# A Mamba mixer on one core: decays from two float32r parts, a shorter step-size chain, the skip moved three steps, one buffer for tokens and second norm

## The reference

```
mod = (silu(c) @ wmod) -> sa, ca, ga, sb, cb, gb      # per sequence, 256 each
h   = layernorm(x) * (1 + ca) + sa
x   = x + ga * attn(h);   h = layernorm(x) * (1 + cb) + sb
x   = x + gb * ffn(h)

attn(h):  xn = layernorm(h) * ln_w + ln_b              # the second norm
          z, xBC, dt = split(xn @ in_proj_w)           # 512, 768, 32 columns
          dt  = softplus(dt + dt_bias)                 # the step size, 32 heads
          xBC = silu(causal_conv(xBC, 4 taps));  x_ssm, B, C = split(xBC)
          # per head h, over time t:
          state = state * exp(dt*A) + dt * outer(x_ssm, B);   y = state @ C
          y = (y + D_skip * x_ssm) * silu(z)           # the skip
          y = y * rsqrt(mean(y^2)) * rms_w;  out = y @ out_proj_w + h
          out = out + relu(layernorm(out) @ m1 + b1) @ m2 + b2
```

## Time and profile before

| | |
|---|---|
| median of 3 runs | 3185.61 us |
| the profiled execution, its own time | 3180.88 us |
| its span | 3179.2 us |
| mean granted TensorE clock | 0.943 of full |
| TensorE busy over the span | 2799.2 us (88%) |
| VectorE busy | 1839.9 us (58%) |
| ScalarE busy | 1384.6 us (44%) |
| GpSimd busy | 678.1 us (21%) |

### The profile page before, as it was taken

The page is one execution under the profiler, slowest core; times in us unless marked ns, Lnnn a source line. Parts: engine busy times, 40 slices in busy tenths (PEclk is TensorE's granted clock), DMA queues, the critical chain, the costliest instruction groups (busy, mean ns, idle before and its releaser), DMA issues. The chain is left out here.

```text
span 3179.2 us, 46142 instructions
## 1 busy us (share of the span) xinstructions
PE 2799.2 (88%) x16998; PEld 2086.3 (66%) x16998; DVE 1839.9 (58%) x3504; ACT 1384.6 (44%) x2394; POOL 678.1 (21%) x716
## 2 busy tenths in 40 slices
PE   0488888888888888869999799999999999999999
PEld 0354555455555555458888687887878787878787
DVE  4688888888888888746767433333333333333332
ACT  0566666666666666536555322222222222222221
POOL 5022222222222222210000122222222222222221
PEclk6799989998999899879999899999999999999999
DMA  3010101010101010035211100000000000000000
GB/s 125 29 35 20 35 20 35 20 35 20 35 21 35 21 35 11 28 104 208 70 62 64 48 13 7 11 14 16 14 16 14 16 14 16 14 16 14 16 14 8
DMA packets 104858, 107.06 MB, mean 34 GB/s; under 512 B 35897, under 2 KB 98617, under 8 KB 102977
## 3 DMA queue, kind: packets, MB, share of 16 engines
q1 hardware_dynamic: 99520, 103.81, 10.1%
q10 hardware_dynamic: 5120, 0.19, 0.1%
HBM read 71.41 MB, written 40.94 MB: 35 GB/s over the span
## 5 line engine op out<-in xcount | busy, mean ns | idle before, releaser
L1597 PE MATMUL fbank<-hid,fw 128*128 128x512 f32 x4096 | 962.3, 395 | 0.0
L1597 PEld LDWEIGHTS fbank<-hid,fw 128*128 128x128 f32 x4096 | 766.1, 187 | 187.0
L1747 DVE TENSOR_TENSOR hid<-fhf,hid 128x512 fp32r<-128x512 f32 x384 | 264.9, 690 | 704.3 <-POOL hid L1704 704.3
L1704 POOL TENSOR_SCALAR hid<-fhf 128x512 fp32r<-128x512 f32 x384 | 271.1, 706 | 1040.2 <-ACT fhf L1676 760.8
L808 ACT ACTIVATE mh<-ebank 128x512 f32<-128x512 f32 x512 | 302.0, 598 | 415.0 <-PE ebank L663 413.8
L1121 DVE SCALAR_TENSOR_TENSOR mh<-mh,gm 128x512 f32<-128x512 f32 x512 | 403.2, 794 | 1.8 <-ACT mh L808 1.8
L663 PE MATMUL ebank<-cright,cleft 102*128 102x512 bf16 x512 | 211.1, 413 | 64.1 <-ACT cin L847 28.9
L1676 ACT ACTIVATE fhf<-fbank,sh2c 128x512 f32<-128x512 f32 x128 | 88.0, 688 | 382.4 <-PE fbank L1597 382.4
L676 PE MATMUL yin<-mh,xpad 128*32 128x128 f32 x4096 | 230.5, 300 | 27.1 <-DVE mh L1121 26.6
L650 PE MATMUL ebank<-ah,win 128*128 128x512 f32 x640 | 246.7, 425 | 7.1 <-ACT cin L847 6.6
L1676 ACT ACTIVATE fhf<-fbank,sh1c 128x512 f32<-128x512 f32 x128 | 88.1, 688 | 320.8 <-PE fbank L1597 320.6
(11 more groups left out here) (180 smaller groups left out, 4380.1 us busy)
## 6 DMA issues: line engine op xcount, KB each, us to landing
fx<-x_d SPq DMA_DIRECT2D x17, 512.0 KB, 3.9
xs<-in_x SPq DMA_DIRECT2D x16, 512.0 KB, 4.3
h_d<-in_h SPq DMA_DIRECT2D x16, 512.0 KB, 5.4
o_d<-o SPq DMA_DIRECT2D x16, 512.0 KB, 2.9
mo<-o_d SPq DMA_DIRECT2D x16, 512.0 KB, 3.8
mx<-in_x SPq DMA_DIRECT2D x16, 512.0 KB, 4.8
x_d<-mx SPq DMA_DIRECT2D x16, 512.0 KB, 2.8
fw<-h_d SPq DMA_DIRECT2D x2, 4096.0 KB, 15.2
```

The lines of the kernel that those rows point to most:

```text
L1597: mm = pe.matmul(bank[banks.slot(key)][:], w[:, k, m * P:(m + 1) * P].bitcast(dt), h[:, k, :].bitcast(dt), start=(k + n == 0), stop=(k == ...
L1704: pool.tensor_scalar(hid[i % 2][0][:, m, :], hf[j % 3][:], 1.0, 0.0, ALU.mult, ALU.add)\
L1747: dve.tensor_tensor(hid[i % 2][1][:, m, :], hf[j % 3][:], hid[i % 2][0][:, m, :].bitcast(F32), ALU.subtract).then_inc(c_lo.sem, 1)
```

## The change

The decay data have two float32r parts in place of three bf16: `cum` rounded to float32r, and the rest (one copy and one subtraction, where there were five instructions). `pick`, `cleft` and `cright` become float32r with 64, 69 and 69 rows in place of 96, 102 and 102, and the constant for masked exponents is -32768. The DMAs into them are 8 per block and 2 per chunk in place of 12 and 3, of 512 bytes a row in place of 256. GpSimd writes the constants once in float32, and ScalarE copies them into the float32r tiles. `chain` has 17 steps in place of 20. `skip` runs at i = 6 of its own chunk, not at i = 3 of the next. The second norm is written over the tokens (`nrm = xs`), so a load waits until TensorE's transposes of the norm before have been read out.

```diff
-LEFT = 99 + P // STRIP - 1
-NEVER = -30000.0
+LEFT = 2 * NH + 2 + P // STRIP - 1
+NEVER = -32768.0
-CHAIN = SERIES + 13
+CHAIN = SERIES + 10
-    pick = sb("pick", [96, QI, P], BF16)
-    cleft = [sb(f"cleft{j}", [LEFT, NC, P], BF16) for j in range(2)]
-    cright = [sb(f"cright{j}", [LEFT, NH, P], BF16) for j in range(2)]
+    pick = sb("pick", [2 * NH, QI, P], F32R)
+    cleft = [sb(f"cleft{j}", [LEFT, NC, P], F32R) for j in range(2)]
+    cright = [sb(f"cright{j}", [LEFT, NH, P], F32R) for j in range(2)]
@@ prologue, scalar
+            act.wait_ge(s_fill, FILLED)
+            nc.scalar.activation(pick[:], pick_f[:], ACT.Copy)
+            for j in range(2):
+                nc.scalar.activation(cleft[j][:], left_f[:].unsqueeze(1).to_broadcast([LEFT, NC, P]), ACT.Copy)
+                nc.scalar.activation(cright[j][:], right_f[:], ACT.Copy)
@@ prologue, gpsimd
-            for j in range(3):
-                v = pick[:].rearrange("k q (h d) -> k (q h) d", d=HD)
+            v = left_f[2 * NH:LEFT, :]
+            pool.affine_select(out=v, in_=v, compare_op=ALU.is_ge, fill=0.0, base=STRIP,
+                               pattern=[[1, P]], channel_multiplier=-STRIP)
+            v = right_f[2 * NH:LEFT, :, :]
+            pool.affine_select(out=v, in_=v, compare_op=ALU.is_ge, fill=NEVER, base=STRIP,
+                               pattern=[[0, NH], [1, P]], channel_multiplier=-STRIP).then_inc(s_fill, 1)
+            for j in range(2):
+                pool.wait_ge(s_fill, 3 + j)
+                v = pick_f[:].rearrange("k q (h d) -> k (q h) d", d=HD)
                 pool.affine_select(out=v, in_=v, compare_op=ALU.not_equal, fill=1.0, base=-NH * j,
                                    pattern=[[-1, NH], [0, HD]], channel_multiplier=1)
-                for r in range(2):
-                    v = cright[r][0:96, :, :]
-                    last = pool.affine_select(out=v, in_=v, compare_op=ALU.not_equal, fill=-1.0,
-                                              base=-NH * j, pattern=[[-1, NH], [0, P]], channel_multiplier=1)
...
+                v = right_f[0:2 * NH, :, :]
+                pool.affine_select(out=v, in_=v, compare_op=ALU.not_equal, fill=-1.0, base=-NH * j,
+                                   pattern=[[-1, NH], [0, P]], channel_multiplier=1).then_inc(s_fill, 1)
-    nrm = sb("nrm", [P, NC, D])
+    nrm = xs
-    parts = [sb(f"parts{r}", [P, 3, P], BF16) for r in range(2)]
+    parts = [sb(f"parts{r}", [P, 2, P], F32R) for r in range(2)]
@@ mixer, sync
+                if i + 2 < BLOCKS:
+                    released(sp, ("nT", i + 1, KD - 1))
+                    load(i + 2)
                 decay_right(NC * i + 2)
...
-                if i + 3 < BLOCKS:
-                    sp.wait_ge(c_norm.sem, c_norm.at(0, i + 3))
-                    load(i + 3)
@@ mixer, scalar
-                if i == 3 and has_chunk(q - 1):
-                    skip(q - 1)
+                if i == 6 and has_chunk(q):
+                    skip(q)
@@ mixer, vector, chain
                 elif step == SERIES + 8:
                     mark(dve.tensor_copy(p_[:, 0, :], cum[:]))
-                elif step == SERIES + 9:
-                    mark(dve.tensor_tensor(crest[:, 0, :], cum[:], p_[:, 0, :], ALU.subtract))
-                elif step == SERIES + 10:
-                    mark(dve.tensor_copy(p_[:, 1, :], crest[:, 0, :]))
-                elif step == SERIES + 11:
-                    mark(dve.tensor_tensor(crest[:, 1, :], crest[:, 0, :], p_[:, 1, :], ALU.subtract))
                 else:
-                    dve.tensor_copy(p_[:, 2, :], crest[:, 1, :]).then_inc(c_cum.sem, 1)
+                    dve.tensor_tensor(p_[:, 1, :], cum[:], p_[:, 0, :].bitcast(F32), ALU.subtract)\
+                        .then_inc(c_cum.sem, 1)
```

More of the change, by code:

```diff
@@ L314, in mixer @@
     h_mh = Handover(sem, "mh", groups, MH)
-    h_left = Handover(sem, "cleft", list(blocks), 2, fills=16 * 3 * NC, both=False)
-    h_right = Handover(sem, "cright", list(chunks), 2, fills=48, both=False)
+    h_left = Handover(sem, "cleft", list(blocks), 2, fills=16 * 2 * NC, both=False)
+    h_right = Handover(sem, "cright", list(chunks), 2, fills=32, both=False)
     c_yread = Count(sem, "yin_read", 0)
@@ L467, in _ @@
             pool.memset(tri[:], 1.0)
[L468 to L472, removed]
+            pool.memset(pick_f[:], 0.0)
+            pool.memset(left_f[:], 1.0)
+            pool.memset(right_f[:], 0.0).then_inc(s_fill, 1)
             pool.wait_ge(s_fill, 1)
@@ L478, in _ @@
             pool.wait_ge(s_fill, 2)
-            for j in range(3):
-                v = pick[:].rearrange("k q (h d) -> k (q h) d", d=HD)
+            v = left_f[2 * NH:LEFT, :]
[7 more added lines that the diff above has]
+                v = pick_f[:].rearrange("k q (h d) -> k (q h) d", d=HD)
                 pool.affine_select(out=v, in_=v, compare_op=ALU.not_equal, fill=1.0, base=-NH * j,
                                    pattern=[[-1, NH], [0, HD]], channel_multiplier=1)
-                for r in range(2):
-                    v = cright[r][0:96, :, :]
-                    last = pool.affine_select(out=v, in_=v, compare_op=ALU.not_equal, fill=-1.0,
-                                              base=-NH * j, pattern=[[-1, NH], [0, P]], channel_multiplier=1)
[L487 to L498, removed]
+                v = right_f[0:2 * NH, :, :]
+                pool.affine_select(out=v, in_=v, compare_op=ALU.not_equal, fill=-1.0, base=-NH * j,
+                                   pattern=[[-1, NH], [0, P]], channel_multiplier=1).then_inc(s_fill, 1)
+            pool.wait_ge(s_fill, FILLED)
     xs = sb("xs", [P, NC, D])
@@ L595, in decay_right @@
                     made(sp, ("eb", q - 2, NG - 1))
-                for j in range(3):
-                    sp.dma_start(cright[q % 2][96 + j:97 + j, :, :],
-                                 parts[q // NC % 2][NH * (q % NC):NH * (q % NC) + NH, j, :])\
+                for j in range(2):
+                    sp.dma_start(cright[q % 2][2 * NH + j:2 * NH + j + 1, :, :].bitcast(F32),
+                                 parts[q // NC % 2][NH * (q % NC):NH * (q % NC) + NH, j, :].bitcast(F32))\
                         .then_inc(h_right.full(q), 16)
@@ L605, in decay_left @@
                 for c in range(NC):
-                    for r in range(3):
-                        sp.dma_start(cleft[j % 2][NH * r:NH * (r + 1), c, :],
-                                     parts[j % 2][NH * c:NH * (c + 1), r, :]).then_inc(h_left.full(j), 16)
+                    for r in range(2):
+                        sp.dma_start(cleft[j % 2][NH * r:NH * (r + 1), c, :].bitcast(F32),
+                                     parts[j % 2][NH * c:NH * (c + 1), r, :].bitcast(F32)).then_inc(h_left.full(j), 16)
             load(0)
[L611 to L616, removed]
+            released(sp, ("nT", 0, KD - 1))
+            load(1)
+            decay_left(0)
+            decay_right(0)
             for i in blocks:
                 decay_right(NC * i + 1)
+                if i + 2 < BLOCKS:
+                    released(sp, ("nT", i + 1, KD - 1))
+                    load(i + 2)
                 decay_right(NC * i + 2)
@@ L685, in state_decay @@
                 for f in range(QI):
[L686 removed]
+                    mm = pe.matmul(o[:, f * P:(f + 1) * P], pick[:, f, :], cleft[q // NC % 2][0:2 * NH, q % NC, :],
                                    start=True, stop=True)
@@ L1190, in _ @@
                         low(j, AL_AT.index(n))
-                    if 0 <= n - CHAIN_FROM < CHAIN // CHAIN_PER:
-                        for step in range(CHAIN_PER):
-                            chain(j, CHAIN_PER * (n - CHAIN_FROM) + step)
+                    for step in range(CHAIN_PER * (n - CHAIN_FROM), CHAIN_PER * (n - CHAIN_FROM + 1)):
+                        if 0 <= step < CHAIN:
+                            chain(j, step)
                     if n == WV_AT:
```

5 lines of the change are left out of this document (4 added, 1 removed).

## The result

The changed kernel takes 3280.57 us, median of 4 runs (3278.43 to 3283.45), against 3186.28 us in the same session: 1.0289 times as long, 95% interval 1.0267 to 1.0312. It is slower by 94 us; 14.7 were forecast.

The account below looks back on a forecast made before the run. TensorE, with ScalarE's readings in its loop, was taken to pace the blocks. Terms -15 - 1 - 24.8 - 4.2 + 38.7 + 3 + 5 + 11 + 2 = +14.7 on 3185.6 gave 3200 us, range 3160 to 3232.

Parts of the forecast that it names:

- Prologue, -15: Before the blocks: fewer GpSimd selects let VectorE's small instructions and the split of `w_in` run faster, saving 15 us.
- Skip, its price: Steps 6, 14 and 22: the skip delays ScalarE's readings, 1.29 us each; +38.7 for 6 and 14, +3 for 22.
- The wait for `cin`: Sign at the exponent products: TensorE waits near 2.25 us, 30 times, some 65 us in all where it was 28.9.
- Skip, its gain: Block ends and starts: waits tied to the skip go, 1.65 us per end (-24.8) and 0.28 per start (-4.2).
- Float32r decays, +16: TensorE in the blocks: longer weight loads, +5 at steps 0, 4 and 5, +11 for `state_decay` at 9, 17 and 25.
- Rival C: Blocks: products of 128 columns at float32's price, +22, 3222 us, or more low-clock stretches; chance 0.18.
- B: Rival, TensorE's weight loads: they hide behind other products, so no change, 3184 us; chance 0.12.
- The clock, no price: Mixer: longer waits at steps 6 and 14 could bring more stretches at 1.2 GHz; nothing for it in the sum.
- Blocks with the waits filled: Sign in the mixer: blocks take 1.9 us longer than before.
- A: Rival, blocks: VectorE sets the pace, TensorE's slack swallows the skip's 38.7 us, 3162 us; chance 0.20.
- D: Rival, block ends: the wait for TensorE's `intra` replaces the skip's, the 24.8 us go, 3225 us; part of Rival C's chance.

Follow-up runs that it names:

- E2: Kernel before the change with only the skip moved to i = 6 of its own chunk; 3207.1 us.
- E5: Changed kernel, with TensorE repeating the transpose of B eight times more at steps 6, 14 and 22, results unused; 3221.2 us.
- E4: Kernel before the change, bf16 parts kept, with constants written once in float32 and copied by ScalarE, and the skip at i = 5 of its own chunk; 3119.9 us.
- E10: Kernel before the change with only the constants written once in float32 and copied by ScalarE; 3177.2 us.
- E11: E3 with ten float32r products of unused result at step 29, where TensorE waits for the Silu; 3211.3 us.
- E7: E4 with ten float32r products of unused result at step 29, where TensorE waits for the Silu; 3143.3 us.
- E1: Changed kernel with the skip put back at i = 3 of the next chunk; 3220.1 us.
- E3: Changed kernel with the skip at i = 5 of its own chunk, one step earlier; 3197.9 us.
- E8: E4 with the second norm written over the tokens and the changed kernel's order of loads of x; 3121.9 us.

## Why the prediction was wrong

TensorE's steps, from one exponent product to the next, in us, even block 6 and odd block 7 of each profile; some steps are left out, `all` is the whole block:

```
step    before      E2          after       E5          E4
  0   5.74  6.56  5.49  5.39  6.39  6.41  5.89  5.38  4.60  5.14
  5   3.11  3.11  2.89  2.89  4.64  2.89  2.89  2.89  2.89  2.88
  6   2.24  2.24  3.39  3.39  3.40  3.40  3.40  3.40  2.24  2.24
  7   2.18  2.18  2.18  2.55  4.04  2.29  2.29  2.29  2.18  2.18
  8   3.32  3.32  3.32  4.49  4.49  3.33  3.33  3.33  3.32  3.32
  9   2.17  3.25  2.17  3.25  2.26  3.74  2.27  3.74  2.17  3.25
 14   2.24  2.24  3.39  3.39  3.40  3.40  3.40  3.40  2.24  2.24
 15   2.18  2.32  3.63  3.47  2.58  2.29  2.30  2.29  2.18  2.18
 16   3.32  3.32  3.35  3.56  4.57  3.32  3.33  3.33  3.32  3.32
 22   1.57  1.57  2.72  2.72  2.73  2.73  2.74  2.73  1.57  1.57
 23   2.18  2.18  2.18  2.18  3.77  2.29  2.29  2.29  2.18  2.18
 24   4.57  4.57  3.43  3.43  3.32  3.33  3.32  3.33  4.56  4.65
 30   3.38  3.38  1.93  1.93  1.97  1.97  1.97  1.97  1.93  1.93
 all  76.8  79.3  78.7  81.7  88.7  82.0  79.6  80.9  74.0  76.1
```

- **Prologue, -15.** Right: 15 by E10, 16.7 in the profile, for the reason given.
- **Skip, its price.** Right in place and nearly in size: 1.15 at steps 6 and 14 (1.29 forecast), and at step 22 the 1.15 comes back at step 24, where the wait for `yg` gave way. The wait for `cin` is 2.1 us and 59 us in all by the rows of the products, 2.4 and 66 by those of the weight loads (2.25 and 65 forecast).
- **Skip, its gain.** Right at the end of a block (step 30: 1.45 for 1.65) and too small at the start: with the skip at 6 alone (E2), step 5 gives 0.22 and step 0 another 0.25 and 1.17, for 0.28 in all. With the skip at 5 step 0 gives 1.1 to 1.4: there the low stretch of the block's end is over earlier as well, and low clock takes 9 us a block in place of 13.
- **Float32r decays, +16.** Too small. The 0.11 us of the longer load stands at step 4, as forecast, and not at 5, but at 7, 15, 19, 21 and 23 too, and `state_decay` costs 0.5 at steps 9 and 17 and 0.42 at 25 where 0.25 was forecast; steps 24, 26 and 28 give some of it back. (It runs at step 1 as well, where nothing grew, and not at step 9 of even blocks, where a sequence begins; the prediction counted 9, 17 and 25 of every block.) Its rows in after, of one group at step 25, answer to the earlier trace rows:

```profile
782.26 0.52 PEld L685 LDWEIGHTS ebank<-cleft,pick 64*128 64x128 f32 x4 [0.20 <-issue]
782.26 0.66 PE L685 MATMUL ebank<-cleft,pick 64*128 64x128 f32 x4
```

  The four loads take 0.29 us more than the bf16 ones, from the first product to what follows the four it is 0.59 us for 0.23, and the steps are 0.42 to 0.5 longer. Undisturbed blocks say 1.8 us in all (E11 against E7), 27 us, not 16. Rival C had the direction, but the steps grew by up to 0.25 us more than my value and not by 0.49; B falls, for the loads show, and the 0.20 us of "issue" is there again.
- **The clock, no price: the step that failed.** The prediction wrote that longer waits "could bring more such stretches. I put no price on that in the sum", and gave C 22 us for all of it. It is the largest term. E5 takes the stretches behind the three waits away, leaves the waits, and is 59 us below after and 28 above before; 14.7 were forecast for just that kernel. Some 11 of the rest are the float32r term (27 for 16); the remainder is not told apart. The step table gives the price: against E5, an even block of after takes 2.9 us more at steps 7 and 8, 1.5 at 15 and 16 and 1.5 at 23, 5.9 us behind the three waits, and 2.7 more at steps 3 to 5; step 0 takes 0.5 and 1.0 more. That is 9.1 us in an even block and 1.1 in an odd one. Blocks 6 and 7 of after differ by 6.7 only, since odd blocks take 1.9 us more at steps 9 to 11, in E5 as well. The 41 us or so of the three stretches are what a price on longer waits would have had to hold. The rest came along with them, and which of the changed parts brings it is open: E1 and E3 have such stretches without a longer wait.
- **Blocks with the waits filled** are near the forecast, in part by luck: the later pairs of E5 take 80.2 us a block for 78.5 before, 1.7 longer (1.9 forecast). The float32r term was 0.7 us a block too small, and the gain at the start of a block about as much.
- **A**, VectorE as the one that paces, falls: steps 6 and 14 grew by nearly the whole skip (1.15 of 1.26), and VectorE's wait for `yin` grew (16.8 to 41.8 us), so that VectorE waits more for TensorE, not less. **D** falls with it: that wait did take the place of the one for `dx`, but the end of a block still gained its 1.45 us.

The Trainium skill, page "TensorE: Matmul & The Clock Gate", section "HAM oscillation — how this bites in real kernels", tells of a kernel whose clock falls at each wait for a DMA between two bursts of products. The traces agree, and add that it needs no DMA and no long wait: 2.1 us of waiting for ScalarE in a step of 3.4 can do it. What is not settled is why the same wait costs a stretch in block 6 and none in block 7 (by E10 timing has a part in it), and why the float32r decays, which keep TensorE busier, come with the stretch at steps 3 to 5 so much oftener.

E4 is the version to keep: the skip at step 5, constants once, bf16 parts. E8 is as fast and needs one buffer less.

## What to carry to other kernels

Work moved on an engine goes where that engine waits for the bottleneck, not merely ahead of its deadline: the same four instructions at step 5 save 55 us, at step 6 they cost 17. A wait that is added to TensorE costs its own length and, where it is added to one already there, perhaps a stretch at half the clock behind it, which here was about as much again (in after 5.9 us in every second block, for waits that cost 2.3 us in each); look for the granted clock behind every wait that is to grow, and give it a price in the sum. And filling a wait with products of no use is a good test of this, and a remedy only where TensorE, and not another engine, sets the pace behind the wait.

## What the chip showed that was not expected

- A wait of 2.1 us, where the 0.96 us before had no low stretch behind it, changed the clock for the next two steps, in every second block: 8.5 us for the products of steps 7 and 8 in place of 5.6.
- Eight products without use in each of three waits of a block made a kernel 59 us (1.8%) faster.
- The effects don't add: skip at step 6 +17 (E2), all but the skip +30 with the prologue's gain in it (E1), together +94.
- A float32 select on GpSimd of 4096 elements a row takes 3.82 us, as the bf16 one did. Float32r weight loads of 64 rows take 0.19 us each at the full clock where bf16 of 96 rows take 0.10.
